# A four-layer graph network on one core: groups of eight gathers, four in flight or one

## What is computed

```python
edge_index = jnp.stack([src, dst])
x = _layernorm(x + _L0_gnn_ref(x, edge_attr_16, ..., src, dst))     # softmax over edges of one destination
x = _layernorm(x + _L1_gnn_ref(x, edge_index, W_tp, weight, bias))  # sum by source, then bilinear
x = _layernorm(x + _L2_gnn_ref(x, edge_index, eps1, w1a, ...))      # two convolutions with
...                                                                 # agg = segment_sum(x[src], dst)
x = _layernorm(x + _L3_gnn_ref(x, src, dst, edge_type_8, ...))      # m = segment_sum(edge_emb[type] @ x[src], dst), GRU
```

## Time and profile before

| | us |
|---|---|
| timed executions, median of 3 (range) | 4963.42 (4960.14 to 4969.88) |
| span of the profiled execution (no other time is recorded for it) | 6039.6 |
| PE busy, share of the span | 3233.3, 54% |
| DVE busy | 3478.9, 58% |
| ACT busy | 1662.3, 28% |
| POOL busy | 3283.8, 54% |
| POOL in the 1,176 gathers of the three passes (L700) | 802.5 + 402.4 busy |
| mean granted TensorE clock | 0.72 |

### The profile page before, as it was taken

The page is one execution under the profiler, slowest core; times in us unless marked ns, Lnnn a source line. Parts: engine busy times, 40 slices in busy tenths (PEclk is TensorE's granted clock), DMA queues, the critical chain, the costliest instruction groups (busy, mean ns, idle before and its releaser), DMA issues. The chain is left out here.

```text
span 6039.6 us, 55665 instructions
## 1 busy us (share of the span) xinstructions
PE 3233.3 (54%) x12357; PEld 2386.3 (40%) x12357; DVE 3478.9 (58%) x5668; ACT 1662.3 (28%) x4307; POOL 3283.8 (54%) x2775
## 2 busy tenths in 40 slices
PE   7999999973444429981002562001555100187786
PEld 3444444443444428871002541001543100177743
DVE  8999999988555528881013861102877200156678
ACT  4666666643111104441000111000112100022234
POOL 5777777763888878887773006775000577500100
PEclk9999999996555559995555676555666555566698
DMA  3111111114343331211000021000003100000012
GB/s 100 41 46 44 46 41 46 44 36 115 60 59 58 60 41 49 56 45 15 6 6 3 0 61 36 6 6 4 0 19 85 29 7 6 4 1 1 1 52 64
DMA packets 373578, 211.63 MB, mean 35 GB/s; under 512 B 105770, under 2 KB 343662, under 8 KB 373442
## 3 DMA queue, kind: packets, MB, share of 16 engines
q1 hardware_dynamic: 254162, 190.55, 11.0%
q0 software_dynamic: 119296, 19.68, 5.4%
HBM read 151.70 MB, written 58.34 MB: 35 GB/s over the span
## 5 line engine op out<-in xcount | busy, mean ns | idle before, releaser
L1190 PE MATMUL ps<-arena 128*128 128x128 f32 x2976 | 647.5, 402 | 1456.4 <-issue 983.8
L700 POOL DMA_INDIRECT extra<-x_t,srci x784 | 802.5, 1024 | 794.7 <-issue 781.8
L1190 PEld LDWEIGHTS ps<-arena 128*128 128x128 f32 x2976 | 597.1, 304 | 1493.7 <-issue 1482.0
L1635 DVE TENSOR_TENSOR arena<-ps,relp 128x1024 f32<-128x1024 f32 x186 | 226.6, 1218 | 956.0 <-remote 664.0
L1094 PE MATMUL ps<-edge_in,wl 17*128 17x512 f32 x784 | 701.9, 1072 | 18.5 <-DVE arena L1436 7.2
L700 POOL DMA_INDIRECT extra<-h_t,srci x392 | 402.4, 1027 | 527.2 <-issue 527.2
L687 POOL DMA_INDIRECT sums<-cmb,sidx x392 | 613.6, 1565 | 136.6 <-issue 120.2
L928 ACT ACTIVATE ps<-extra 128x16 f32 x1392 | 163.3, 169 | 1568.5 <-issue 939.0
L649 POOL DMA_INDIRECT xg<-in_x,xidx x392 | 480.4, 1226 | 210.0 <-issue 116.0
L636 POOL DMA_INDIRECT ft_t<-fts,fidx x392 | 507.4, 1294 | 143.4 <-issue 120.3
L1661 DVE TENSOR_TENSOR arena<-arena,ps 128x128 f32 x1488 | 426.0, 286 | 236.5 <-issue 55.1
(11 more groups left out here) (204 smaller groups left out, 6318.4 us busy)
## 6 DMA issues: line engine op xcount, KB each, us to landing
edge_in<-far_row SPq DMA_DIRECT2D x98, 256.0 KB
ain<-in_src_row SPq DMA_DIRECT2D x56, 448.0 KB
sums<-zero SPq DMA_DIRECT2D x132, 144.0 KB
arena<-rel_t SPq DMA_DIRECT2D x63, 256.0 KB
x_t<-yout SPq DMA_DIRECT2D x28, 448.0 KB, 3.3
xin<-x_t SPq DMA_DIRECT2D x28, 448.0 KB, 4.3
extra<-x_t,srci POOLq DMA_INDIRECT x784
ain<-x_t SPq DMA_DIRECT2D x28, 448.0 KB, 4.6
```

The source lines that it names most:

```text
L700: pool.indirect_dma_start(dy[:, t, :], None, table, bass.IndirectOffsetOnAxis(ap=srci[:, t:t + 1], axis=0)).then_inc(d_gathered[n % QUEUE] ...
L1190: last = pe.matmul(slot_sums(k, n)[:, j * P:(j + 1) * P], oneh[b][:, j * P:(j + 1) * P], placed[b][:, j * P:(j + 1) * P], start=True, stop ...
L1635: dve.tensor_tensor(by_slot(oneh[c % 2]), io_p.unsqueeze(1).broadcast_to((P, SG, P)), relp[:, bass.ds((2 * i + c) * SG, SG)].unsqueeze(2). ...
```

## The change

It sets the constant `QUEUE` from 4 to 1.

```diff
@@ -68,7 +68,7 @@
 SG = 8
 SLOT_GROUPS = -(-(COLS + BLOCKS - 1) // (2 * SG)) * 2
 TILE_GROUPS = COLS // SG
-QUEUE = 4
+QUEUE = 1
 SQ = -(-SLOT_GROUPS * SG // P)
 SN = SQ * P
 DST_PASSES = 3
```

## The result

The change takes **5208.57 us** (median of four runs, 5205.16 to 5210.32), the kernel before, timed beside it, 4962.17 (4960.14 to 4969.88). The ratio is 1.0494, 95% interval 1.0482 to 1.0507: 246 us slower. The forecast was 5224, in a range of 5135 to 5310.

What follows compares the result with a forecast made beforehand. The prediction took POOL's issue of gathers to bound each pass. It added 144 x 1.85 = 266 us to 4963.4, giving 5229, lowered to 5224 for pass 2's thin margin, with a range of 5135 to 5310.

Steps and rivals of the forecast that it cites:

- a round trip: Before each group's first gather: landing plus POOL's start, gap 2.15 us instead of 0.30, costing 1.85 us at 144 places.
- The landing of 1.4 us: Between groups: 1.4 us from the end of the eighth gather's issue to SP's first relay.
- the last group's 2.1 us: Last gather of all: relay 2.1 us after its issue's end, thought special to its tile of padded edges.
- the ends of the passes: Slot work after each pass's gathers: stays as it is, cost 0; without holds 15, 15 and 90 us.
- POOL's start after the relay: Step at each group's start: POOL released and its gather started, taken as 0.75 us, bounds 0.30 to 0.95.
- its signs: Changed profile: gap before each group 2.0 to 2.3 us, period near 11.9 us early in a pass.
- the timed runs have no holds: Gather stretches: DVE's 39 us holds are only in the profiled execution; removals sum to 1129 against 1076 us required.
- rival B: Gather stretches: timed runs have DVE holds, each POOL pause ends one, so the change is faster, 4391 us; chance 0.04.
- The 53 us that the sum lacked: Profiled span without holds and late-gather excess: 4911 us, 53 short of the timed median.
- pass 2's thin margin: Pass 2: steps of 9.8 us against 10.0 of gathers; an 11 us step would hide 48 us of cost.
- rival A: Pauses partly hidden by pass 2's steps or paid back by late gathers: 5076 at lowest, or 5181 us; chance 0.13.
- the late gathers' excess of 105 us: Late in each pass: wider gather spacing adds some 35 us, three times 105, taken as absent from timed runs.

Runs made afterwards that it cites:

- e4: The change, with POOL waiting on the gathers' own semaphore instead of SP's relay: 5444.50 us, ratio 0.9027 to the kernel before.
- e8: The change, with POOL also waiting for the first four gathers of each group before issuing the other four: 5419.17 us, ratio 0.8986 to the kernel before.
- e1: The kernel before with two groups of gathers in flight instead of four (QUEUE = 2): 6031.75 us, ratio 0.9991.
- e12: The change, with one POOL memset ahead of each group in all passes and pass 2's type mask in PSUM: 5223.72 us, ratio 0.8658 to the kernel before.
- e5: The change itself, run again on a chip where the kernel before takes 6033.85 us: 5347.45 us, ratio 0.8878.
- e7: The change's wait, but for only seven of the last group's gathers, the eighth having its own semaphore pair: 6011.82 us, ratio 0.997 to the kernel before.
- e6: The kernel before, four groups in flight, with three POOL memsets of an unread buffer after each group: 5653.36 us, ratio 0.9408.
- e11: The change, with one POOL memset of an unread buffer ahead of each group in passes 0 and 1: 5245.36 us, ratio 0.8693 to the kernel before.
- e9: The kernel before, four groups in flight, with six POOL memsets of an unread buffer after each group: 5328.67 us, ratio 0.8828.
- e3: The kernel before, four groups in flight, with pass 2's type mask in PSUM instead of SBUF: 6038.82 us, ratio 1.0009.
- e2: The change, with pass 2's type mask in PSUM instead of SBUF: 5548.73 us, ratio 0.9208 to the kernel before.
- e10: The kernel before with one group in flight in pass 2 alone, four in passes 0 and 1: 5676.66 us, ratio 0.9407.

## Why the prediction came out as it did

**Right: what the kernel pays.** POOL's gathers set the length of a pass in the runs that were timed at first, each group pays a round trip, 144 times, and nothing hides it. The landing of 1.4 us, from the earlier trace rows, is 1.4 us in the changed profile. SP's relay is almost free (e4), the last group's 2.1 us is no price of the others, the ends of the passes are 22, 22 and 93 us against 15, 15 and 90 expected, and 147 more waits cost 1.43 us each (e8).

**Mis-sized: POOL's start after the relay.** The step took 0.75 us from the starts of the passes. It is 0.28 us, just below the lower bound of 0.30. So the gap is 1.7 us and the period 11.4, where the prediction named 2.0 to 2.3 and 11.9 as its signs. Those rows compared SP and POOL at the start of a pass, after two waits each on other semaphores, and measured POOL's own way to its first gather, not a wake: at the start of pass 0 POOL's wait (L693) is over 0.8 us before that gather starts. It made the sum 144 x 0.47 = 68 us too large.

**Missed: pass 2's first gather.** The change brings POOL's gather and DVE's spread to the same relay, and the spread holds the gather for 0.94 us. That is 48 x 0.94 = 45 us which the sum didn't have. That DVE waits for the relay (L1625) was known from the description of the kernel; what the two do to each other when they start together was not asked. The two errors nearly cancel: 266 - 68 + 45 = 243. That the forecast of 5224 fits to 15 us owes something to that, and this part is luck.

**Right once, and not in general: "the timed runs have no holds".** From 6039.6 against 4963.4 the prediction concluded that holds belong to the profiled execution. The changed profile, which is a timed execution without holds, agrees with the 4962 us having none; no profile shows that directly. But the conclusion on why was wrong: the profile of before and its timed runs are of two kinds of the same kernel, and on four chips (e1 to e12) the timed runs take 6032 to 6037 us and so have the holds. There the change is 11% faster (e5), and rival B, given 0.04, is the right account of the mechanism: pauses of POOL let the slot work pass. It said 4963 - 4391 = 572 us gained; e5 gained 686. One detail of it is narrower: a pause of 0.4 us ends nothing (e7), one of 1.5 to 1.7 us for each group ends a part of the holds (e6, e5), and one of 2.0 or more (e11, e12, e9) or two of 1.7 (e8) end all.

**The 53 us that the sum lacked.** They were put down to pass 2's thin margin (rival A). The changed profile is against that: its passes take 586, 588 and 704 us, 1878 together, so the kernel before had 1878 - 246 = 1632 in them, against 3 x 490 + 138 = 1608 by a sum without any excess of late gathers. The 24 us left are near what the ten pauses of 3.2 us would add, 10 x 2.9 = 29. Shown is only that the late gathers' excess of 105 us was not there in full; that the pauses were is inferred. On the other four chips the excess is there when the gathers come without a pause, and gone when they don't: the mean gather takes 1.00 to 1.03 us in e1, e3 and e7, as in the profile of before, and 0.94 to 0.95 in passes 0 and 1 of e5, e6 and e9.

**What stays open.** What holds the engines, and why the same kernel has the holds in one place and not in another. The fetches of instructions that rival B named are not more where the holds are: beside the gathers of pass 0 the DMA queue for instructions has 3 packets in the profile of before and 3 in that of the change, of 0.53 and 0.48 us in the mean. How long an engine waited for one, the profile doesn't say. The length of POOL's pause after eight gathers is shown as the condition: with none or 0.4 us (a period of 10.0 us early in a pass, 10.7 in the mean) nearly all slot groups are held, with 1.5 to 1.7 us (11.3 to 11.4) a part, with 2.0 us or more (11.7) none. What of it acts is not separated: in every kernel that frees slot groups the rate is lower and the queue of gathers runs empty before the next group (0.1 to 0.2 us before it in e6, 0.28 in e5, 0.64 in e11, 1.6 in e9, and twice some 0.3 in e8), and in every kernel that frees none it doesn't. A memset of 0.3 us or so after every single gather would lower the rate and, with gaps well under the 1.4 us of a landing, keep the queue filled. That would tell the two apart; it wasn't run. At 11.4 us the share also varies (40, 42 and 30 beside the gathers in e2, 47 and 49 in e5, and 60 beside the 4962 us). Neither e3 nor e12 was run where the kernel before takes 4962 us.

## What to carry to other kernels

A wait for a landing on the engine that issues the gathers costs a whole landing each time, 1.4 us here, while a depth of two groups was as good as four, and one gather more in flight already hid nearly all of it: on a bound issuer, ask how many issues fit into one landing. When a change ties two engines to one semaphore, look at what their next instructions share. And when a profile's span and the timed median differ by a fifth, don't reason the difference away as the profiler's: time the kernel again elsewhere before trusting the sign of any change that slows down or paces the busy engine.

## What the runs showed of the hardware that was not expected

- Engines are slow to go on from instruction to instruction while another issues gathers without a pause (ACT's copies each 1.40 us instead of each 0.1), in some places and not in others: the same kernel takes 4962 or 6032 to 6037 us, and the change 5209 or 5347. An instruction of 0.42 us that does nothing made a kernel of 5347 us one of 5245 (e11).
- A gather's issue that starts 0.17 us after a DVE instruction with two SBUF inputs takes 1.88 us instead of 0.94; with one of them in PSUM, 0.94 (e2).
- POOL starts its gather 0.28 us after SP's relay, and 0.24 us after the landing where it waits for that itself (e4).
- POOL pauses for 3.2 us after every 113 gathers in the kernels with one semaphore and one group in flight, and not in pass 2 of e10, with one group in flight and four semaphores.
